# Three buffers for the gate activations, and the last two LayerNorm squares moved from ScalarE to VectorE

## The reference

```python
def _rfs(xw, ab, AB, gs):
    dot_products = einsum('...d,rd->...r', xw, ab[:, None] * gs)
    correction = (0.5 * sum(xw * xw, axis=-1))[..., None] * (ab * ab)
    return 1.0 / sqrt(1024) * AB * exp(dot_products - correction)
# layer: x is (2, 8192, 1024), xis and all dims 1024, hidden 3072
weights = _rfs(input_weights, xis, exp(xis), proj_matrix)
feats   = _rfs(x, xis, exp(xis), proj_matrix)
x = layernorm(x + einsum('bsr,or->bso', feats, weights))
gate = einsum('bsd,hd->bsh', x, w_gate / 127)      # w_* are integers of -127..127
up   = einsum('bsd,hd->bsh', x, w_up / 127)
x = layernorm(x + einsum('bsh,dh->bsd', silu(gate) * up, w_down / 127))
```

## Time and profile before

| | us |
|---|---|
| two runs without the profiler | 741.06 and 762.56, median 751.81 |
| the profiled execution's own time | 740.86 |
| its span on the slowest core (core 1) | 739.3 |
| spans of the eight cores | 735.9 to 739.3 |
| PE busy on core 1 | 701.8 |
| ACT, DVE busy on core 1 | 199.4, 181.3 |
| mean granted TensorE clock, by core | 0.988 to 0.990 of full speed |

### The profile page before, as it was taken

How to read it: one execution, slowest core, us unless ns; L and a number is a source line. 1 busy time by engine, 2 the same in 40 slices (tenths; PEclk the granted TensorE clock), 3 DMA queues, 4 the chain that set the end, 5 groups by cost and what they waited for, 6 DMA issues and landing times.

```text
span 739.3 us, 9046 instructions; the slowest of 8 cores (735.9 to 739.3 us)
## 1 busy us (share of the span) xinstructions
PE 701.8 (95%) x3424; PEld 314.2 (43%) x3424; DVE 181.3 (25%) x325; ACT 199.4 (27%) x326; POOL 9.1 (1%) x21
## 2 busy tenths in 40 slices
PE   2999999999959999999999999999999999999994
PEld 0333435353424444444444444444444444444442
DVE  1120334252522221131321112221122131211221
ACT  1222336252542111043311104231110523111122
POOL 2000000000000000000000000000000000000000
PEclk9999999999988999999999999999999999999998
DMA  8991030871084000001200000120000100000011
GB/s 119 167 354 43 2 57 1 202 312 58 1 358 154 0 1 1 1 28 58 86 0 1 1 1 29 58 86 0 1 0 2 55 31 29 0 1 1 1 58 57
DMA packets 5835, 44.63 MB, mean 60 GB/s; under 512 B 800, under 2 KB 800, under 8 KB 3104
## 3 DMA queue, kind: packets, MB, share of 16 engines
q0 software_dynamic: 2192, 27.27, 13.4%
q1 hardware_dynamic: 3600, 16.78, 6.0%
HBM read 30.42 MB, written 12.58 MB: 58 GB/s over the span
## 4 chain that ended last, share of the span: by engine, by line
PE 92%; DMA 3%; DVE 2%; ACT 2%; issue 1%; POOL 0%; DVEq 0%; ACTq 0%; SPq 0%; POOLq 0%
PE pt L629 23%; PE P L591 22%; PE P L687 22%; PE P L275 8%; PE P L435 5%; PE P L322 4%; DMA bfarena<-projT 2%; PE P L280 1%; PE pt L468 1%; PE P L693 1%; PE P L703 1%; PE P L441 1%; PE P L447 1%; PE pt L240 1%; DVE bfarena L366 1%
## 5 line engine op out<-in xcount | busy, mean ns | idle before, releaser
L591 PE MATMUL P<-bfarena 128*128 128x512 bf16 x768 | 185.6, 383 | 0.0
L629 PE MATMUL pt<-bfarena 128*128 128x512 bf16 x768 | 181.8, 379 | 0.0
L687 PE MATMUL P<-bfarena 128*128 128x512 bf16 x736 | 163.2, 379 | 0.0
L642 DVE SCALAR_TENSOR_TENSOR bfarena<-pt,bfarena 128x512 bf16<-128x512 f32 x96 | 66.4, 692 | 246.6 <-PE pt L629 239.6
L610 ACT ACTIVATE bfarena<-P 128x512 bf16<-128x512 f32 x96 | 57.3, 597 | 230.9 <-PE P L591 230.4
L591 PEld LDWEIGHTS P<-bfarena 128*128 128x128 bf16 x768 | 75.4, 98 | 93.4 <-issue 3.5
L629 PEld LDWEIGHTS pt<-bfarena 128*128 128x128 bf16 x768 | 74.9, 98 | 92.5
L687 PEld LDWEIGHTS P<-bfarena 128*128 128x128 bf16 x736 | 71.9, 98 | 88.7
L366 DVE TENSOR_SCALAR_CACHE_REDUCE bfarena<-P 128x1024 bf16<-128x1024 f32 x32 | 39.2, 1225 | 200.5 <-PE P L703 144.7
L275 PE MATMUL P<-bfarena 128*128 128x512 bf16 x256 | 63.4, 390 | 4.2 <-DMA bfarena<-projT 4.2
L393 ACT ACTIVATE f32arena<-f32arena 128x1 f32<-128x1 f32 x32 | 9.4, 295 | 170.9 <-DVE f32arena L385 169.9
(11 more groups left out here) (56 smaller groups left out, 244.5 us busy)
## 6 DMA issues: line engine op xcount, KB each, us to landing
out<-f32arena SPq DMA_DIRECT2D x16, 512.0 KB, 2.6
bfarena<-wgT POOLq DMA_DIRECT2D x1, 6144.0 KB, 53.5
bfarena<-wdT POOLq DMA_DIRECT2D x3, 2048.0 KB, 13.1
bfarena<-wuT POOLq DMA_DIRECT2D x1, 4608.0 KB, 26.4
x1s<-bfarena SPq DMA_DIRECT2D x4, 1024.0 KB, 4.3
bfarena<-x1s SPq DMA_DIRECT2D x4, 1024.0 KB, 5.6
bfarena<-xfm POOLq DMA_DIRECT2D x3, 1024.0 KB, 14.2
bfarena<-projT POOLq DMA_DIRECT2D x2, 1024.0 KB, 19.2
```

What stands on the lines that cost most here:

```text
L591: return e.matmul(pg, bf(WGT_O + dk * 3072 + hc * 128, 128), bf(xb1 + dk * 512, 512), start=(dk == 0), stop=(dk == DK - 1))
L629: return e.matmul(puj, bf(wu_off + hc * 128, 128), bf(xb1 + dk * 512, 512), start=(dk == 0), stop=(dk == DK - 1))
L642: "vector", "VE", lambda e, j=j, hc=hc, puj=puj: e.scalar_tensor_tensor(hact_ap(hc, 0, 512), puj, 1.0 / 16129.0, sg_ap(j), OP.mult, OP.mult))
L687: e.matmul(P1[:, base + oh * 512:base + oh * 512 + 512], hact_ap(hc, m * 128, 128), bf(reg + (hc % 8) * 1024 + oh * 512, 512), start=(hc = ...
```

## The change

It has two edits. The first takes out the special case of the blocks 14 and 15 for the square: their heads now make it on DVE like all others (L378), and their tails on ACT lose L392. The application of these two stays on DVE.

The second gives `sg_ap` a third buffer. A Silu now waits for the `ve_h` of three chunks before it and no longer for that of two before. With it, in the handoff, Silu 2 is emitted right behind gate 2, ahead of the tail of block 15, and Silu 3 behind up 0 in place of up 1. (In this diff `hc` is the chunk; the loop over hc < 4 holds the transposes, the gates and the tails.)

```diff
-BF_END = WUT1_O + 18432
+SG3_O = WUT1_O + 18432
+BF_END = SG3_O + 512
...
             em.inc("vector", "VE", lambda e, negS=negS, negm=negm: e.tensor_scalar_mul(
                 negm, negS, -1.0 / 1024.0))
-            if phase == 0 and i >= 4 * NT - 2:
-                return
             if phase == 0 and i >= 4:
                 em.wait("vector", "MM", ev["mm_tr", i - 4])
...
             em.wait("scalar", "VE", vv0)
-            if phase == 0 and i >= 4 * NT - 2:
-                em.wait("scalar", "MM", ev["mm_tr", i - 4])
-                em.inc("scalar", "SE", lambda e, dv=dv, s2=s2,
-                       out_ap=out_ap:
-                       e.activation(out_ap, dv, AF.Square, accum_out=s2))
             em.inc("scalar", "SE", lambda e, s2=s2, t2a=t2a, t2=t2: e.activation(
                 t2, s2, AF.Identity, bias=t2a))
...
         def sg_ap(j):
-            return bf(SWROW_O + (j % 2) * 512, 512)
+            k = j % 3
+            return bf(SG3_O, 512) if k == 2 else bf(SWROW_O + k * 512, 512)
...
                 em.wait("scalar", "MM", ev["mm_g", j])
-                if j >= 2:
-                    em.wait("scalar", "VE", ev["ve_h", j - 2])
+                if j >= 3:
+                    em.wait("scalar", "VE", ev["ve_h", j - 3])
...
                     emit_tr(NT - 1, hc)
                     emit_gate(pi, hc, mm_only=True)
-                    if hc < 2:
+                    if hc < 3:
                         emit_silu(pi, hc)
                 for hc in range(4):
                     emit_up(pi, hc)
-                    if hc < 2:
-                        emit_silu(pi, hc + 2)
+                    if hc == 0:
+                        emit_silu(pi, 3)
```

## The result

| | before | changed |
|---|---|---|
| plain runs, median (us) | 741.1 (8 runs) | 748.22 (9 runs, 747.09 to 750.61) |
| ratio to before | | 1.0096, 95% interval 1.0083 to 1.0109 |
| profiled execution (us) | 740.86 | 747.09 |
| spans of the eight cores | 735.9 to 739.3 | 742.8 to 745.5 |
| mean of the eight spans | 737.6 | 744.1 |

The change makes the kernel slower by 1.0%, some 7 us. That is inside the 2% band but clear of noise.

The account below looks back on a forecast made before the run. PE, busy 95% of the span, was taken as the bound, with reachable waits in the handoff between phases. On 740.86 us, +1.34 +0.6 -1.24 +4.40 +0.8 made +5.9, so 746.8 us, range 742 to 754.

Parts of the forecast that it names:

- the base: Whole kernel: the profiled execution's 740.86 us, to which the forecast terms were added.
- the clock term: Transposes 14 to gate 3, perhaps into up 0: PE's lower clock after stalls costs 0.8 us more than before.
- The store later by 1.34: Before transposes 13: block 14's square on DVE delays SP's store and the copy of block 12, +1.34 us.
- Its meeting with the loads: Before transposes 13: the later store overlaps the first weight loads on the DMA engines, +0.6 us.
- The square off the path of 14: Stall before transposes 14: without the square on ACT it shrinks from 5.68 to 4.44 us, -1.24 us.
- The tail of 15 behind Silu 2: Stall before transposes 15: ACT's queue and an extra table load raise it from 1.34 to 5.74 us, +4.40 us.
- The third buffer at nothing: Feed-forward: waiting for three chunks before removes a wait that never came last, 0 us.
- the clock that never falls: Rival, transposes 14 to gate 3: full clock through both stalls, -3.6 for +0.8, total 742.4 us; chance 0.10.
- The store caught in full: Rival, before transposes 13: store queues behind weight loads, landing 13.3 us later, total 759.5 us; chance 0.05.
- The third rival: Handoff: both tails get shorter and the new order costs little, about 740 us; chance 0.03.

Follow-up runs that it names:

- e5: e1 with block 14's square moved behind the copy of block 11 in DVE's queue; 737.58 us, ratio 0.9959 to the kernel before.
- e8: The changed kernel with the three down-projection weight loads issued behind the end of gate 1; 745.41 us, ratio 1.0066 to the kernel before.
- e1: The changed kernel with only the order of Silu 2 and 3 put back, behind up 0 and up 1; 740.43 us, ratio 0.9996 to before.
- e2: The kernel before with only the third buffer and the new Silu order, squares of 14 and 15 on ACT; 746.71 us, ratio 1.0083.
- e7: The changed kernel with 48 unread extra products on PE ahead of transposes 13, 14 and 15; 741.99 us, ratio 1.0020 to before.
- e3: The kernel before with only the third buffer, Silu order unchanged; 741.41 us, ratio 1.0008.
- e9: e6 with two buffers and the old places of Silu 2 and 3; 732.04 us, ratio 0.9862 to the kernel before.
- e10: The kernel before with only the ACT tails of 14 and 15 ahead of Silu 0, DVE's applications behind copies 12 and 13; 731.25 us, ratio 0.9854.
- e6: The changed kernel with block 14's square behind the copy of block 11 and both ACT tails ahead of Silu 0; 730.51 us, ratio 0.9866 to before.

## Why the prediction was right in its mechanism, and where it failed

Two steps failed: the base, which made the sign of the forecast depend on which number of before one takes, and the clock term, forecast at +0.8 us and measured at +1.67. The waits and their order were right, and the forecast difference of +5.9 us stands against +6.2 in the profiled executions and +7.1 in the medians. The forecast time of 746.8 was 1.4 us short of the 748.22. In the handoffs' means the growth is 6.65, so the terms are 0.75 short: 0.87 on the clock and 0.17 on the tail of 15, against 0.21 and 0.08 the other way on the store's meeting and the square. That the total came out so near is in part this cancelling.

**The base.** The sum was made against the profiled 740.86. The same section set the 762.56 aside as a run apart, but never named the median then shown, 751.81 of two runs. As a time, 746.8 lies below that median and says "faster", while the text says "0.8% more". Eight runs put before at 741.1, so the base was the right one, and the kernel did get slower than that; but the forecast should have said in so many words which of the two numbers its sign refers to.

**The store later by 1.34** is exact: 1.34 measured, and e5 takes it away by moving one operation. **Its meeting with the loads**, 0.6, is 0.39 (e8): the direction held, but the 0.6 was half of a rough upper bound, so that it came near is luck, and what I had not seen is that the landing was 0.26 longer already before. Together the stall before 13 grew by 1.73 in the mean, where 1.94 was forecast.

**The square off the path of 14**, -1.24, is 4.35 - 5.67 = -1.32. **The tail of 15 behind Silu 2**, +4.40, is 5.91 - 1.34 = +4.57. The rows under the 5.91 are those that the prediction named. e1 takes 5.4 of it away, and e2 shows it without edit 1. The rule of the Trainium skill, page "ScalarE: Activation LUTs", section "Rules for kernel authors", to do all of one table set before switching, fits this result, as far as the switch goes: two of the 1.28 us loads stand in that stall. By the drain of about 1380 ns that the section "What ACT_TABLE_LOAD costs" of that page of the Trainium skill adds to a load, the stall would be 5.74 + 1.38 = 7.1 us, an estimate; it is 5.91, and Silu 2 starts 1.29 us after its load.

**The clock** was the mis-sized term: +0.8 forecast, 4.79 - 3.12 = +1.67 in the mean. It went wrong at both ends. The 3.6 of core 1 was taken as before's cost, but four of the eight cores paid only 2.3 each (worked out for each core as in the table), and the mean is 3.1. And 3.6 + 0.8 = 4.4 was forecast for the changed kernel, where all eight pay 4.6 to 4.9. The prediction let only the stalls before 14 and 15 bring the clock down; on three cores it fell already after the stall before 13, which the prediction itself had growing to 3.5 us but left out of this term. That this time is really on the path is shown by e7, which gives 4.5 us back by making PE work more.

**The third buffer at nothing** agrees with e3 in the old order and with e9 with the tails first.

Of the rivals, the clock that never falls did not happen: it fell in every core of the changed kernel. The store caught in full did not happen either; its landing moved by 0.4 us and not by 13.3. The third rival's 740 us is what e1 measures, with the old order: it was right about the parts and wrong in that the new order costs little. The forecast was 5.74 for the last stall, and it is 5.91.

The sum of the measured terms, +1.73 - 1.32 + 4.57 + 1.67, is +6.65, which is the growth of the handoff.

## What to carry to other kernels

When an instruction is moved up in the queue of an engine that works in order, look at what it waits for and at what then stands behind that wait. Here a Silu waited for a product, and a LayerNorm on which PE depended stood behind it; a free buffer made that order possible without making it good. Before a handoff, finish the work that shares a function table and is ready (the tails) ahead of the first operation of the other table. When a tuned kernel loses time in stalls, write down for each of them the last wait and the place of its releaser in its queue; e10 needed only that, and no faster operation.

## What the runs showed of the hardware

The same stall was followed by half clock on some cores and by full clock on others. Behind the 2.11 us before the transposes 13, five cores of e9 and one of e6 ran gate 1 wholly or in part at half clock, the other ten at full clock. Core 3 of e9 and core 0 of e6, in this order:

```profile
210.00 0.61 PE L477 MATMUL pt<-bfarena 128*128 128x128 bf16 x8 [2.11 <-DVE bfarena L493]
210.45 3.51 PE L600 MATMUL P<-bfarena 128*128 128x512 bf16 x8
```

```profile
209.03 1.91 PE L602 MATMUL P<-bfarena 128*128 128x512 bf16 x8
```

No stall before the transposes 13 of up to 1.85 us did it, on any core (before, e2 to e5, e10), while of the 2.90 to 3.34 us in the changed kernel it followed on three cores of eight. So a stall's length alone did not say whether the clock falls. Where it fell in e6 and e9 it cost 1.6 us (handoffs of 19.82 against 18.25).

It is also new to me that 48 products whose results nobody reads can shorten a program. Between e7 and the changed kernel they, and one wait ahead of them for a buffer of P1, are the only difference in PE's queue.
